# A graph layer's last stage with the self terms added by TensorE and copied by ScalarE, and ScalarE laying out the second list

## The reference, cut to what matters

```
h = relu(layernorm(x))
msg = concat(h[dst], h[src] - h[dst]) @ W.T + b
x = x + segment_max(msg, dst)          # 0 where a node has no edge
```

## Time and profile before

| | |
|---|---|
| median of 3 runs | 879.14 us (876.09 to 879.84) |
| the profiled execution | 878.57 us, of which the span is 876.9 us |
| DVE busy | 801.8 us, 91% of the span |
| POOL / PE / ACT busy | 71% / 62% / 47% |
| mean granted TensorE clock | 0.862 |

### The profile page before, as it was taken

The page is one execution under the profiler, slowest core; times in us unless marked ns, Lnnn a source line. Parts: engine busy times, 40 slices in busy tenths (PEclk is TensorE's granted clock), DMA queues, the critical chain, the costliest instruction groups (busy, mean ns, idle before and its releaser), DMA issues.

```text
span 876.9 us, 8002 instructions
## 1 busy us (share of the span) xinstructions
PE 547.9 (62%) x2442; PEld 264.7 (30%) x2442; DVE 801.8 (91%) x1290; ACT 408.1 (47%) x244; POOL 619.9 (71%) x631
## 2 busy tenths in 40 slices
PE   2564896000000468777777767788888888888852
PEld 1553565000000123322233323333333333333331
DVE  7989999999999799998899899999999998888985
ACT  3786213000039055775675769755555756351000
POOL 2677277887777767777777777777777677777742
PEclk9999999555555599998899888999999999999985
DMA  8951003323364665665554556555656654453655
GB/s 261 204 150 25 8 21 94 90 59 92 86 194 97 182 194 174 175 171 137 174 157 149 171 138 175 173 179 170 185 172 193 217 193 150 148 176 79 95 108 166
DMA packets 114694, 126.75 MB, mean 145 GB/s; under 512 B 19542, under 2 KB 96836, under 8 KB 114379
## 3 DMA queue, kind: packets, MB, share of 16 engines
q1 hardware_dynamic: 95090, 86.33, 32.3%
q0 software_dynamic: 19376, 38.94, 18.6%
q10 hardware_dynamic: 184, 0.96, 0.3%
HBM read 86.43 MB, written 40.57 MB: 145 GB/s over the span
## 4 chain that ended last, share of the span: by engine, by line
DVE 33%; PE 17%; issue 13%; DMA 1%; ACT 1%; POOL 0%; DVEq 0%; POOLq 0%; SPq 0%
DVE acc L1291 19%; PE ps L852 17%; DVE maxima L1235 10%; DVE hT L1244 2%; DVE hT L1258 1%; DMA ohs<-winners 1%; ACT ohs L598 1%; DVE hT L1249 1%; DVE hT L1349 1%; DMA hT<-running_max,end_row 0%; DMA running_max<-maxima 0%; POOL hT L705 0%; POOLq L197 0%; DVEq L1290 0%; DVE hT L1351 0%
## 5 line engine op out<-in xcount | busy, mean ns | idle before, releaser
L726 POOL DMA_INDIRECT rows<-near_table,idx x503 | 516.5, 1027 | 181.2 <-issue 134.6
L1291 DVE TENSOR_TENSOR acc<-ps,acc 128x1924 f32<-128x1924 f32 x196 | 344.1, 1780 | 34.7 <-PE ps L852 34.4
L852 PE MATMUL ps<-ohs,near 128*128 128x481 fp8e3 x1404 | 319.3, 381 | 77.4 <-DVE acc L1291 68.9
L598 ACT ACTIVATE ohs<-ohs,spike 128x6272 fp8e3<-128x6272 uint8 x36 | 197.8, 5513 | 82.3 <-DMA ohs<-winners 82.3
L852 PEld LDWEIGHTS ps<-ohs,near 128*128 128x128 bf16 x1404 | 134.2, 100 | 262.5 <-DVE acc L1291 88.9
L1235 DVE SCALAR_TENSOR_TENSOR maxima<-maxima,fresh,rows 128x128 f32<-128x128 f32 x503 | 176.4, 351 | 13.7
L593 ACT ACTIVATE hT<-k,off 128x1600 bf16<-128x1600 int16 (+6 forms) x49 | 65.9, 1392 | 205.8 <-DVE hT L1249 182.8
L852 PE MATMUL ps<-sorts_mem,near 128*128 128x481 fp8e3 x507 | 117.7, 387 | 28.6 <-DVE acc L1291 26.7
L840 PE MATMUL ps<-flags,ones 128*128 128x10 f32 x2 | 0.6, 360 | 150.3 <-DVE spare L1269 150.3
L598 ACT ACTIVATE sorts_mem<-sorts_mem,spike 128x6272 fp8e3<-128x6272 uint8 x13 | 71.7, 5515 | 23.2 <-DMA sorts_mem<-winners 23.2
L852 PEld LDWEIGHTS ps<-sorts_mem,near 128*128 128x128 bf16 x507 | 49.4, 102 | 96.6 <-DVE acc L1291 31.1
(11 more groups left out here) (182 smaller groups left out, 461.7 us busy)
## 6 DMA issues: line engine op xcount, KB each, us to landing
running_max<-maxima SPq DMA_DIRECT2D x63, 512.0 KB, 3.7
ohs<-winners SPq DMA_DIRECT2D x36, 784.0 KB, 6.5
sorts_mem<-winners SPq DMA_DIRECT2D x13, 784.0 KB, 6.5
rows<-near_table,idx POOLq DMA_INDIRECT x503, 3.2
acc<-in_x SPq DMA_DIRECT2D x6, 512.0 KB, 7.2
near_table<-acc SPq DMA_DIRECT2D x12, 256.0 KB, 4.5
base<-in_x SPq DMA_DIRECT2D x1, 2744.0 KB
out_x<-hT SPq DMA_DIRECT2D x12, 224.0 KB
```

The costliest lines, as they stand in the source:

```text
L598: nc.scalar.activation(oh[t % OHS], oh_bytes[t % OHS], ACT.Abs_reciprocal_sqrt, bias=spike[:, 0:1], scale=float(SPIKE), saturate=False).th ...
L726: nc.gpsimd.indirect_dma_start(rows[:, n % (SLOTS * GATHERS), :], None, near_table[:, :], bass.IndirectOffsetOnAxis(idx[:, n:n + 1], 0)).t ...
L852: last = nc.tensor.matmul(bank(4 * (n % 2) + c - UNITS[r][0])[:, 0:CHUNK], near[:, t, part, :], oh[t % OHS][:, at:at + CHUNK], start=part ...
L1291: V.tensor_tensor(into, found[:, 0:z - a, 0:CHUNK], into, ALU.max).then_inc(max_done, 1)
```

## The change

Two things are changed, and the planner's numbers with them.

**The second list.** `loser_words` is split: `first_words` does for columns 0 to 14 what was done before, and `second_words` does columns 15 to 48 with other arithmetic. ACT writes each column's sorted numbers, plus the column number, into `numbers` in column order (34 instructions of 64 elements, with a bias from `j_bias`), behind `k2_ready`. DVE multiplies the two flag arrays in place as int16 (`loser_bits`), and ACT lays the result out by column as float, scaled to a step of the shift (`stays`). DVE's scan then gives the shift itself, no longer a count that must be subtracted from a number and shifted.

**The end.** PE transposes into eight banks. For the first 11 groups DVE's join is the maximum alone; PE then adds `rowsF` and `base` with two float32 products by the identity into the group's bank, and ACT copies the bank to `rowsF`. Groups 11 and 12 keep DVE's add. `CUTS` has a fourth part: columns 44 to 46 are fetched when step 495's block is stored.

```diff
-CUTS = ((36, 400), (44, 472), (49, 504))
+CUTS = ((36, 400), (44, 472), (47, 496), (49, 504))
...
-    pieces += [("flags", cost, 1.8) for cost in (2.05, 2.6, 2.5, 2.5, 3.9, 0.1)]
-    pieces += [("words", cost, 1.8) for cost in (5.0, 4.2, 5.3, 2.05, 3.0)]
+    pieces += [("flags", cost, 1.8) for cost in (2.05, 2.6, 2.5, 2.5, 1.4)]
+    pieces += [("words", cost, 1.8) for cost in (6.0, 3.0, 1.2, 3.0)]
...
-            pieces += [("round", (2.15, 1.65, 1.65, 1.65)[r], 1.3)]
+            pieces += [("round", (2.15, 1.65, 1.65, 1.65)[r], 1.26)]
...
@@ scalar
+            a, z, _ = PARTS[1]
+            numbers, at = words[1][1], LEFT + (z - a) * KS
+            act.wait_ge(k2_ready, 1)
+            for j in range(a, z):
+                last = nc.scalar.activation(numbers[:, LEFT + (j - a) * KS:LEFT + (j - a + 1) * KS], S1[:, :, j], ACT.Identity,
+                                            bias=j_bias[:, j:j + 1])
+            last.then_inc(numbers_ready, 1)
+            act.wait_ge(losers_known, 1)
+            nc.scalar.activation(picks[1][:, LEFT:at].rearrange("p (j k) -> p j k", k=KS),
+                                 loser_bits.rearrange("p k j -> p j k"), ACT.Identity, bias=one_step[:, 0:1],
+                                 scale=-float(1 << SHIFT_AT)).then_inc(stays_ready, 1)
...
+            for g in range(summed_groups):
+                a, z = spans[g]
+                act.wait_ge(sum_made, g + 1)
+                nc.scalar.copy(rowsF[:, a:z, :], bank(g % 8)[:, 0:(z - a) * D].rearrange("p (j d) -> p j d", d=D)).then_inc(final_ready, 1)
...
@@ tensor
+            def turn(g):
+                a, z = spans[g]
+                if g >= 8:
+                    pe.wait_ge(final_ready, g - 7)
                 for j in range(a, z):
-                    last = nc.tensor.transpose(bank(g % 4)[:, (j - a) * D:(j - a + 1) * D],
+                    last = nc.tensor.transpose(bank(g % 8)[:, (j - a) * D:(j - a + 1) * D],
                                                acc[:, j:j + (P - 1) * tiles + 1:tiles], ident[:, :])
                 last.then_inc(accT_made, 1)
+            def add_base(g):
+                a, z = spans[g]
+                pe.wait_ge(joined, g + 1)
+                nc.tensor.matmul(bank(g % 8)[:, 0:(z - a) * D], ident[:, :], rowsF[:, a:z, :], start=True, stop=False)
+                nc.tensor.matmul(bank(g % 8)[:, 0:(z - a) * D], ident[:, :], base[:, a:z, :], start=False, stop=True).then_inc(sum_made, 1)
+            for g in range(groups + 4):
+                if g < groups:
+                    turn(g)
+                if 4 <= g < summed_groups + 4:
+                    add_base(g - 4)
...
@@ vector, loser_flags
+                if h:
+                    V.tensor_tensor(loser_bits, loser_bits, ne[:, :, 0:real], ALU.mult).then_inc(losers_known, 1)
...
@@ vector, second_words
+                then(V.tensor_scalar(stays[:, 0:LEFT], left_real_sb[:, :], -step, step, ALU.mult, ALU.add))
+                then(V.tensor_copy(numbers[:, 0:LEFT], left_sb[:, :]))
...
+                dve.wait_ge(stays_ready, 1)
+                then(V.tensor_tensor_scan(shift, stays, lowest[:, 0:1].to_broadcast([P, at]), -2.0 ** 31, ALU.add, ALU.max))
...
+                dve.wait_ge(numbers_ready, 1)
+                for u, v in in_parts(LEFT, at):
+                    then(V.scalar_tensor_tensor(numbers[:, u:v], stays[:, u:v], -float(IS_LOSER) / step, numbers[:, u:v],
+                                                ALU.mult, ALU.add))
...
@@ vector, join
                 V.tensor_tensor(rowsF[:, a:z, :], found, rowsF[:, a:z, :], ALU.max).then_inc(joined, 1)
-                dve.wait_ge(joined, g + 1)
-                V.tensor_tensor(rowsF[:, a:z, :], rowsF[:, a:z, :], base[:, a:z, :], ALU.add).then_inc(final_ready, 1)
+                if g >= summed_groups:
+                    dve.wait_ge(joined, g + 1)
+                    V.tensor_tensor(rowsF[:, a:z, :], rowsF[:, a:z, :], base[:, a:z, :], ALU.add).then_inc(last_ready, 1)
```

More of the change, by code:

```diff
@@ L121, in schedule @@
         for r in range(4):
[L122 removed]
+            pieces += [("round", (2.15, 1.65, 1.65, 1.65)[r], 1.26)]
         if trees < 25:
[L124 removed]
+            pieces += [(name, cost, 1.3) for name, cost in tree_pieces(trees)]
             trees += 1
@@ L171, in edgeconv @@
     CT = sum(c for _, _, c in PARTS)
-    early_groups, waiting_groups = (cut // GROUP for cut, _ in CUTS[:2])
+    early_groups = CUTS[0][0] // GROUP
+    summed_groups = CUTS[1][0] // GROUP
     spans = [(a, min(a + GROUP, tiles)) for a in range(0, tiles, GROUP)]
@@ L743, in _ @@
                     pool.sem_inc(decided, 1)
-            stored(CUTS[1][1] // STEPS)
-            for g in range(early_groups, waiting_groups):
-                finals(g)
-            stored(all_blocks)
-            for g in range(waiting_groups, groups):
-                finals(g)
+            for (a, _), (z, cap) in zip(CUTS, CUTS[1:]):
+                stored(cap // STEPS)
+                finals(a, z)
         @block.tensor
@@ L883, in _ @@
             then(V.memset(eps[:, :], EPS))
+            then(V.memset(lowest[:, :], -2.0 ** 32))
+            then(V.memset(one_step[:, :], float(1 << SHIFT_AT)))
             then(V.memset(flags[:, :], 0.0))
@@ L983, in _ @@
             then(V.memset(run_at(0), LOW))
+            then(V.tensor_scalar(j_bias[:, :], iota_f[:, 0:tiles], float(1 << J_AT), float(IS_LOSER), ALU.mult, ALU.add))
             settled()
@@ new lines, in first_words @@
+                then(V.tensor_tensor(has[:, 0:n], tot[:, 1:n + 1], tot[:, 0:n], ALU.is_gt))
+                then(V.tensor_scalar(flags[:, 4:5], tot[:, n:n + 1], float(FIRST_CAP - 1), None, ALU.is_gt))
+                then(V.tensor_scalar(end_f[:, a:z], tot[:, 1:n + 1], float(FIRST_CAP - 1), None, ALU.min))
+                then(V.tensor_scalar(left_count[:, :], tot[:, n:n + 1], float(PARTS[0][2]), None, ALU.subtract))
+                settled()
+                for u, v in in_parts(0, at):
+                    then(V.tensor_tensor(words[0][0][:, u:v], words[0][0][:, u:v], words[0][1][:, u:v], ALU.bitwise_or))
@@ new lines, in second_words @@
+                then(V.tensor_scalar(flags[:, 5:6], tot[:, n:n + 1], float(CT - first - 1), None, ALU.is_gt))
+                for c, (cut, most_steps) in enumerate(CUTS[:-1]):
+                    then(V.tensor_scalar(flags[:, 6 + c:7 + c], tot[:, cut - a:cut - a + 1], float(most_steps - first - 1), None,
+                                         ALU.is_gt))
+                for at_cut, (cut, most_steps) in zip([a] + [cut for cut, _ in CUTS], CUTS):
+                    then(V.tensor_scalar(end_f[:, at_cut:cut], tot[:, at_cut - a + 1:cut - a + 1], float(first),
+                                         float(most_steps - 1), ALU.add, ALU.min))
@@ L1155, in loser_words @@
                 yield
+                for u, v in in_parts(0, at):
+                    then(V.tensor_tensor(word[:, u:v], numbers[:, u:v], shift[:, u:v], ALU.bitwise_or))
                 settled()
-                for u, v in in_parts(0, at):
-                    then(V.tensor_tensor(words[h][0][:, u:v], words[h][0][:, u:v], words[h][1][:, u:v], ALU.bitwise_or))
                 then(V.tensor_tensor(cnt[:, 0:n], end_f[:, a:z], has[:, 0:n], ALU.mult))
@@ L1297, in _ @@
                 pass
-            for _ in loser_words(0):
-                pass
+            first_words()
             for _ in compact(0):
```

115 lines of the change are left out of this document (61 added, 54 removed).

## The result

| | before | after |
|---|---|---|
| median of the runs | 879.49 us (876.09 to 880.07) | 869.66 us (869.07 to 870.20) |
| the profiled execution, its span | 878.57, 876.9 us | 869.07, 867.4 us |
| last round ends | 843.3 | 832.8 |
| from there to the end of the span | 33.6 | 34.6 |

The ratio is 0.9897, with a 95% interval of 0.9878 to 0.9916: faster by 9.8 us. The forecast of 876.0 us was too slow, and the time lies under the range. Where a last round ends is read from one profiled execution of each kernel.

A forecast was written before the change was run, and what follows sets the result against it. DVE was taken to bound the kernel up to the last round, then TensorE's additions: 8.3 us won, 5.6 given back, span 876.9 to 874.2, with 1.67 outside 875.9; forecast 876.0 us, own range 872 to 880, overall 871 to 883.

The forecast's parts named there:

- What bounds the kernel: Up to the last round DVE sets the time; at the end the last store takes 4.9 us from issue to span end.
- The list: Second list on DVE: 10.9 us removed, small instructions and a wait for ACT added, 9.8 us taken as the gain.
- the columns: ACT's 34 column instructions of 64 elements in the second list: 0.25 us each, 8.5 us, done before needed.
- the layout: ACT's by-column layout of 2176 elements, before DVE's scan: 2.1 us, with DVE waiting 0.4 to 0.6 us.
- The planner: Four more chain steps in and before the rounds: 1.5 us added, so the last round ends at 834.9.
- The end: Behind the last round: TensorE's additions set the end, 39.3 us instead of 33.7, giving back 5.6 us.
- The start of the additions: TensorE begins adding after 12 chain steps and the first join, 4.6 + 0.7 us behind the last round.
- a short fall: TensorE's clock drops briefly during the additions: four products at 1.2 GHz cost 3.5 us, giving 879.
- count of slow products: In the rival of TensorE's clock down while adding (chance 0.10 throughout, 895): decides from the tenth slow product, 8.6 us.
- Additions cheap or covered: Rival at the end: PE's pair costs 1.0 us, end 11 us earlier, 865, floor 859; chance 0.08.
- The gain on the list doesn't arrive: Rival on the second list: ACT's columns cost more or the chain meets missing gathers; 881, no change; chance 0.17.
- the main case: The forecast itself, list, planner and end summed for the whole kernel: 876.0 us, chance 0.65.

The follow-up runs named there:

- probes: Changed kernel plus three unused ScalarE instructions of 2160 elements (in order, strided read, strided write) and two swapped products where base is made: 869.39 us, one time taken.
- halves: sums0 with the second list's layout and scan split into two halves: 861.87 us, 0.98 of the kernel before.
- new_planner_only: Kernel before with only the planner's two new numbers (1.26 behind a round, 1.3 behind a tree piece): 873.63 us, 0.994.
- old_planner: Changed kernel with the planner's numbers of before (1.3 for rounds, 1.4 for tree pieces): 864.99 us, 0.9841 of the kernel before.
- old_cuts: Changed kernel with three cuts instead of four, columns 44 to 46 fetched behind the last block: 870.96 us, 0.9901 of the kernel before.
- burst: Changed kernel with SP holding the stores of groups 5 to 10 until group 10's sums are copied: 872.87 us in one run.
- early_joins: Changed kernel with two joins also behind the eighth step after the last round: 866.86 us, 0.9864 of the kernel before.
- sums0: Changed kernel with DVE adding the self terms of all 13 groups, none on TensorE: 863.47 us, 0.9827 of the kernel before.
- one_row: Changed kernel with a third product, of one partition, in each pair of the 11 additions: 886.37 us in one run.
- sums4: Changed kernel with TensorE adding for the first four groups only, DVE for the other nine: 864.25 us, 0.9835 of the kernel before.

## Why the prediction was wrong, point by point

*What bounds the kernel.* Right up to the last round. At its end I took the last store for what ended the span; it was POOL's drain, 8.57 us behind the last fetch. The rows on which I relied show issues and no drain, and the waits don't list it.

*The list.* Predicted 9.8 us, measured 7.9. The product took 1.33 us as priced, and the columns took 0.31 us each where I had 0.25, which nothing waited for. The term that was mis-sized is the layout, 2.1 us predicted, 4.15 measured, with a wait of 2.48 us instead of 0.4 to 0.6. probes and halves show it.

*The planner.* I priced the moved steps at full cost, 1.5 us, and put the change of DVE's waits for products at nothing. They fell by 4.2 us (34.4 to 30.2), 1.0 of it by the clock's earlier return. With 7.9 of the list and 1.5 for the steps that makes 10.6; the last round ended 10.5 us sooner, at 832.8, where I had 834.9, and in eight alike kernels at 834.1 in the mean. That the forecast was near is luck: 1.9 us too much for the list and 4.2 us too little for the waits. What I missed is what the planner does to the end: new_planner_only (0.994) and old_planner (0.9841 against 0.9897) show that the same two numbers gain 5 us on the kernel before and lose 5 with TensorE's additions.

*The end.* This is the step that failed, "it takes 39.3 us instead of 33.7". It took 34.6. The start of the additions was right (5.3 us). Of the 4.7 us between the two, 2.3 lie in the additions, 24.3 us from the first to the last sum (838.13 to 862.4) where I had 26.6: a pair costs 1.72 us and not 2.01, no weights are changed at a price, and the transposes of a group take 0.48 and not 0.55; 1.7 us come back by the fall of the clock (838.13 to 842.07 takes 3.94 us, a later group 2.20), which old_cuts, burst and early_joins didn't meet in their additions (22.6 us from the first to the last sum). The other 2.4 lie behind the last copy: 6.8 us predicted, 4.4 measured. There the last group's store was to take 4.9 us to the end of the span; without a drain behind it, it takes 2.6 (864.8 to 867.4). The mechanism was right: the additions set the end, hidden by nothing. Without them it ends at 863.5 (sums0).

*The rivals.* The clock fell for little more than one pair, a short fall such as the prediction allowed for but had not put in its sum; in early_joins and old_cuts it didn't fall. By the rule that I had quoted from the Trainium skill (TensorE: Matmul & The Clock Gate, Part 4: PE-mode transpose) it would be down when the additions begin. The trace agrees in half again: it was still full at 838, behind 20 transposes and 2.4 us of idle time, and was down at 839. In old_cuts, behind the same 20 transposes and wait, it stayed full; in burst it was down among the transposes and full again at the additions. The prediction's count of slow products from which the time would be "slower" is off by one: 7.5 us (876.0 to 883.5) by 0.87 is nine products, not ten. "Additions cheap or covered" had a pair of 1.0 us; it was 1.7. "The gain on the list doesn't arrive" was true by 1.9 us of 9.8. None of them had the time: it came from the main case's sizes. The forecast's own range, 872 to 880, was too narrow for a sum whose end had been priced from two rows and a bound that I had not identified.

*Left open.* The rest of old_planner's advantage over early_joins (2 us, within the intervals), whether TensorE's additions gain 3 us or nothing with the old numbers, why DVE's waits for products differ so much between kernels, and what makes TensorE's clock fall in one execution and not in the next.

## What to carry to other kernels

Ask of the last microseconds which engine's last instruction ends the span, and look at the drains too: here POOL's drain ended 8.57 us behind its last indirect DMA and 2 us behind the last store. Take a duration from a row with the same neighbours and the same order in memory, not only the same size. And an edit that is worth nothing or a loss beside one schedule can gain beside another: cross the parts, all four ways, before one is kept.

## What the runs showed of the hardware

- ScalarE, 2160 elements from int16 to float: 2.08 us in order, 4.26 read in steps of 100 bytes, 4.21 written in steps of 180 bytes.
- TensorE at full clock, float32 products of 512 columns by a 128x128 identity: 0.86 us each behind one another; a product of one partition between them costs 1.25 us.
- POOL's DRAIN ended 8.57 us behind the end of its last indirect DMA in all 17 profiles.
- TensorE's granted clock, behind 20 transposes and a wait of 2.4 us: it fell to 0.50 in the first additions of the changed kernel, probes, one_row and sums4, and not in old_cuts (1.00 from 842 to 846). In burst it was at 0.50 from 834 to 836, during the transposes, which took 4.13 us instead of 2.73.
- The last store was done (SP, which waits for it, goes on) 1.0 to 1.9 us behind the end of its issue in the 17 profiles, and 1.6 us behind it in burst, where eight groups were stored in one piece.
